# A two-layer graph network on one core: the walk over the edges in steps of one tile of 128 instead of two

## The chip, the core and the metric

The kernel runs on one core of a Trainium2 chip. The core has five engines that run side by side and meet through semaphores: TensorE (PE in the profile; PEld is its weight load), VectorE (DVE), ScalarE (ACT), GpSimd (POOL) and SyncE (SP), and 16 DMA engines. The metric is the device time of one execution, in microseconds (us), lower being better.

## The reference

`x` has 6250 rows (nodes) of 256 numbers. There are 200000 edges, sorted by their target node `dst`. Two graph attention layers run over them, and a linear attention ("mix") and a mixture of experts come with them:

```python
def gat_conv(x, W, a_src, a_dst, bias, src, dst, heads, out_ch, concat):
    h = (x @ W).reshape(n, heads, out_ch)
    al_s = jnp.einsum('nhc,hc->nh', h, a_src)
    al_d = jnp.einsum('nhc,hc->nh', h, a_dst)
    logits = jax.nn.leaky_relu(al_s[src] + al_d[dst], NEG_SLOPE)
    m = jax.ops.segment_max(logits, dst, num_segments=n)
    e = jnp.exp(logits - m[dst])
    denom = jax.ops.segment_sum(e, dst, num_segments=n)
    msg = h[src] * (e / denom[dst])[:, :, None]
    out = jax.ops.segment_sum(msg, dst, num_segments=n)
...
xn = _layernorm(x)
x = x + gnn(xn, edges) + mix(xn)          # gnn: gat_conv with 4 heads of 128, prelu, gat_conv with 1 head of 256
x = x + ffn(_layernorm(x))                # top 2 of 8 experts, hidden 1024
```

## The kernel before

The program has five passes, one after the other. `first_pass` normalises `x`, multiplies it by `W1`, and builds the tables of the edge walk. `walk_pass` runs for layer 1 (walk 1, 4 heads, rows of 528 numbers) and, after `finish_layer1`, for layer 2 (walk 2, 1 head, rows of 264 numbers). `finish_layer2` and `expert_pass` end the program.

**The walk's steps.** The nodes are cut into 49 windows of 128 (`NW`). The edge list is cut into blocks of `TPS * 128` edges, and one step of the walk is one block seen from one window: a block that spans the border of two windows is walked twice. So there are `STEPS = BLOCKS + NW - 1` steps. With `TPS = 2` these are 782 + 48 = 830 steps of two tiles of 128 edges. Ten steps (`CS`), that is 20 tiles (`CT`), make a chunk, and there are 83 chunks (`CHUNKS`), so 1660 tiles.

**What a chunk c goes through.** GpSimd gathers the source rows of its 20 tiles into a ring, one indirect DMA for each tile (line 871). The ring holds 2 chunks in walk 1 and 3 in walk 2 (`RS`); a gather waits until TensorE has multiplied the tile that stood in its place. ScalarE copies, for each step, the target window's terms into `goal` (`goals`, line 897); it first loads the ten window numbers of the chunk into registers (`windows_of`, line 714). TensorE spreads these to the edges (line 944). When all rows of chunk c+1 have landed, VectorE takes the maximum with them (`terms`, `walk_best`, line 1195), and a chain of small products and scans between TensorE and VectorE (lines 951 to 1239: `turn_best`, `scan_tiles`, `take_ends`, `scan_ends`, `bring_carry`, `scan_through`, `turn_peaks`, `gaps`) gives the softmax exponents `walk_gap` of chunk c+1. ScalarE turns them into weights and scales three of the four heads of each tile (walk 2: the one head), line 906; VectorE scales the fourth head in walk 1 (line 1260). VectorE also builds `walk_hit`, the 0/1 matrix that says which node of the window an edge belongs to (line 1244), and `walk_hitT` (line 1185).

**Multiply and add.** TensorE multiplies `hit` by the scaled rows of each step and sums both tiles of the step in one PSUM buffer (`multiply`, line 1047), 520 columns wide in walk 1 and 258 in walk 2; there are three such buffers (`PBUF`). VectorE adds each buffer into the accumulator `acc` of the step's window (`add`, line 1277; for the first step of a chunk, in parts with a rescale, lines 1268 to 1275). Each add waits for two semaphores: `multiplied`, for its own product, and `added`, which the add before it increments when it is complete:

```python
def add(c, i, r, s, w):
    b = (r * CS + s) % PBUF
    dve.wait_ge(multiplied, c * CS + s + 1 + AHEAD)
    dve.wait_ge(added, c * CS + s + PBUF)
```

The order of all this work on each engine is written out by hand in `chunk`. While VectorE adds chunk c, it works the chain of chunk c+1 in between. Before the first add of a chunk it loads that chunk's window numbers into registers. In walk 2 the mix (`mix_step`, `mix_products`, `roots`) is interleaved: through the first 50 chunks its keys, then its base rows.

Of the kernel before, what the change touches and what calls it, by code (L numbers as in the profile page):

```python
# [10 lines left out]
ALU = mybir.AluOpType  # L11
# [3 lines left out]
BF16 = mybir.dt.bfloat16  # L15
# [14 lines left out]
TPS = 2  # L30
# [17 lines left out]
CT = CS * TPS  # L48
CHUNKS = -(-STEPS // CS)
# [101 lines left out]
def first_pass(nc, k, d):  # L151


    with ExitStack() as ctx:
# [55 lines left out]
        tables = [a[:, 0:TPS * P] for a in (pF, pE)]  # L210
        XP = 10
        XPARTS = [(c, min(c + XP, NT)) for c in range(0, NT, XP)]
        TABLES = [(j, n) for j in range(SJ) for n in range(3)]
# [36 lines left out]
        with nc.Block() as block:  # L250

            @block.sync
            def _(sp):
# [35 lines left out]
                sp.wait_ge(tables_out, 16 * 10)  # L289
# [51 lines left out]
            def _(dve):  # L341
# [105 lines left out]
                def edge_step(n):  # L447
# [16 lines left out]
                    if n in (6, 7):  # L464
                        for way in range(2):
                            nc.vector.tensor_reduce(through[:, way, :, n - 6], reset[:, :, (n - 6) * P + way:(n - 5) * P + way], AX_X, ALU.min)
                        dve.drain()
                    if n == 7:
                        dve.sem_inc(resets_ready, 1)

                def copy_table(q):
                    j, n = TABLES[q]
                    dve.wait_ge(table_turned, q + 1)
                    steps = slice(j * P, (j + 1) * P)
                    to = (meta[:, 0, steps, :], meta[:, 1, steps, :], index[:, steps, :])[n]
                    nc.vector.tensor_copy(to.rearrange("p s u -> p u s"), tables[q % 2].rearrange("p (u s) -> p u s", u=TPS)
                                          ).then_inc(table_copied, 1)
# [32 lines left out]
            def _(pe):  # L510
# [8 lines left out]
                def edge_work(t):  # L519
# [6 lines left out]
                    if T_TURN <= t < T_TURN + len(TABLES):  # L526
                        q = t - T_TURN
                        j, n = TABLES[q]
# [5 lines left out]
                        for u in range(TPS):  # L534
                            last = nc.tensor.transpose(tables[q % 2][:, u * P:(u + 1) * P], (place, last_one, src)[n][:, j, u * P:(u + 1) * P],
                                                       k["ident"][:, :])
# [25 lines left out]
def walk_pass(nc, k, d, layer, H, A, F, attn, acc, table):  # L562
# [11 lines left out]
    WROW = CS  # L574
# [3 lines left out]
    AHEAD = RS * CS  # L578
    PBUF = 3
    HBUF = 3  # L580
    assert CHUNKS * CS >= STEPS and CHUNKS * CS <= SP
    assert TURN % RS == 0 and TURN % TS == 0 and TURN % IS == 0 and TURN * CS % PBUF == 0 and TURN * CGROUPS % HBUF == 0
    with ExitStack() as ctx:
# [7 lines left out]
        goal = m.sb("goal", [P, CS, 3, 2 * H], BF16)  # L591
# [8 lines left out]
        row_back = m.sb("row_back", [1, RK + 1])  # L600
        carry = m.sb("carry", [RK, 2])
        pair = m.sb("pair", [P, 2, H, CT + 1])
        gap = m.sb("gap", [P, H, CT + 1])
# [108 lines left out]
        def windows_of(engine, r):  # L712

            return nc.values_load_multi_w_load_instructions(win[0:1, r % IS, 0:CS], engines=[engine], min_val=0, max_val=NW - 1,
# [44 lines left out]
        with nc.Block() as block:  # L759

            @block.sync
            def _(sp):
# [5 lines left out]
                def load_tables(c, r):  # L768
# [3 lines left out]
                    sp.dma_start(win[:, r % IS:r % IS + both, 0:CS],  # L772
                                 d["windows"].unsqueeze(0)[:, bass.ds(c * CS, both * CS)].rearrange("o (c s) -> o c s", s=CS)
                                 ).then_inc(tables_ready(r), 16)

                def load_places(n):
                    sp.dma_start(hitT[:, :], d["places"][0:CHUNKS * CS, :].rearrange("(c s) e -> c (s e)", s=CS)[bass.ds(n, 1), :].to_broadcast([W, CT * P])
# [65 lines left out]
                def follow(c, i, r):  # L843
                    after(sp, gap_ready, c + 1)
                    load_resets(c + 2, r)
                    sp.wait_ge(added, c * CS + PBUF)
# [12 lines left out]
                if mixing:  # L859
                    for q in range(XB):  # L860
# [3 lines left out]
            def _(pool):  # L864
                def gather(c, i, r):
                    pool.wait_ge(index_ready(r), index_of(i, r))
                    for s in range(CS):
                        pool.wait_ge(multiplied, c * CS + s + 1)
                        pool.sem_inc(index_seen, 1)
                        for t in range(s * TPS, (s + 1) * TPS):  # L870
# [6 lines left out]
            def _(act):  # L877
# [12 lines left out]
                def goals(n, i, r):  # L890
# [5 lines left out]
                    for s in range(CS):  # L896
                        last = nc.scalar.copy(goal[:, s, :, :], target[:, at[s], :, :])  # L897
                    last.then_inc(goals_in, 1)

                def scale(c, i, r, s):  # L900
                    act.wait_ge(weights_ready, c + 1)
                    for t in range(s * TPS, (s + 1) * TPS):
# [32 lines left out]
            def _(pe):  # L935
                def spread_targets(n, i, r):
# [5 lines left out]
                    for s in range(CS):  # L942
                        for t in range(s * TPS, (s + 1) * TPS):
# [1291 lines left out]
```

## Time and profile before

| what | value |
|---|---|
| median of three runs | 5648.19 us (5645.58 to 5658.97) |
| the profiled execution | 5653.59 us, span 5651.8 us |
| walk 1, first chunk's first add to the last chunk's | 223.7 to 2329.4 us |
| walk 2, the same | 2565.1 to 4647.1 us |
| busy share of the span | PE 77%, PEld 59%, DVE 54%, ACT 53%, POOL 65% |
| gathers | 3320 instructions, 3200.0 us busy |

A row of the timeline gives start, duration, engine, line, operation, output and inputs, shape and count; the bracket is the idle time of the engine just before it and what ended it. "<-issue" is a wait that no event of the profile explains. A row of the waits gives total time, number and longest. "DVEq" is VectorE's own instruction queue, which handles register loads.

### The profile page before, as it was taken

The numbers are of one execution on the slowest core, as the hardware profiler recorded it, in microseconds if no ns is written. First come the engines' busy times: TensorE is split into PE (matmuls) and PEld (weight loads), VectorE is DVE, ScalarE is ACT, GpSimd is POOL, SyncE is SP. The second block draws the span as 40 slices with busy tenths as digits, with TensorE's granted clock in tenths as the row PEclk, the third lists the DMA queues.
The fourth block names the chain that finished last, engine by engine and source line by source line (L and its number), as shares of the span: only waits on it lengthen the run. The fifth ranks groups of instructions, "written<-read, shape, count | busy, mean of one in ns | idle before, by whom it ended". The sixth has DMA issues, their size and how long they took to land. (4 is left out here: it accounts for less than half of the span.)

```text
span 5651.8 us, 82730 instructions
## 1 busy us (share of the span) xinstructions
PE 4335.7 (77%) x21069; PEld 3336.5 (59%) x21069; DVE 3078.8 (54%) x8587; ACT 3010.0 (53%) x10079; POOL 3660.6 (65%) x3778
## 2 busy tenths in 40 slices
PE   7588888888888888775766667666565656899998
PEld 4466666666666666553444444444444435788887
DVE  5477777777777777654545545454454548211111
ACT  2677777777777777674545455453333334122221
POOL 0577777777777777457777777777777762344443
PEclk9789899999999998897778777787777775999999
DMA  5788878888888888435455444444556547443332
GB/s 188 236 242 242 243 234 244 241 243 241 243 243 244 240 243 238 144 119 145 138 143 143 138 144 138 143 140 140 170 159 171 159 119 238 143 129 129 127 127 74
DMA packets 427478, 1021.41 MB, mean 181 GB/s; under 512 B 115224, under 2 KB 207632, under 8 KB 426758
## 3 DMA queue, kind: packets, MB, share of 16 engines
q0 software_dynamic: 229312, 718.64, 44.4%
q1 hardware_dynamic: 197142, 296.44, 15.7%
q8 instruction: 181, 2.97, 0.2%
q14 instruction: 283, 2.32, 0.1%
q10 hardware_dynamic: 560, 1.05, 0.1%
HBM read 952.23 MB, written 65.48 MB: 180 GB/s over the span
## 5 line engine op out<-in xcount | busy, mean ns | idle before, releaser
L871 POOL DMA_INDIRECT walk_ring<-s_h,walk_index x3320 | 3200.0, 964 | 1169.5 <-issue 936.7
L1047 PE MATMUL walk_pM<-walk_ring,walk_hit 128*128 128x262 f32 (+1 forms) x9960 | 2776.8, 431 | 29.6 <-DVE acc L1275 18.0
L1047 PEld LDWEIGHTS walk_pM<-walk_ring,walk_hit 128*128 128x128 f32 x9960 | 2024.2, 211 | 449.9 <-issue 73.5
L906 ACT ACTIVATE walk_ring<-walk_ring 128x128 f32<-128x128 f32 (+1 forms) x6640 | 2134.3, 414 | 5.4
L1277 DVE TENSOR_TENSOR acc<-walk_pM,acc 128x520 f32 (+1 forms) x1494 | 834.3, 558 | 584.9 <-PE walk_pM L1047 564.4
L886 ACT ACTIVATE walk_ring<-walk_gap 128x40 f32<-128x40 f32 (+1 forms) x249 | 54.1, 259 | 1664.9 <-DVE walk_gap L1239 1664.9
L951 PE MATMUL walk_pC<-all_ident,walk_best 128*84 128x128 f32 (+1 forms) x166 | 61.7, 372 | 1032.2 <-DVE walk_best L1195 1032.2
L951 PEld LDWEIGHTS walk_pC<-all_ident,walk_best 128*84 128x84 f32 (+1 forms) x166 | 20.5, 124 | 1094.6 <-issue 1094.6
L1244 DVE TENSOR_TENSOR walk_hit<-walk_pK,walk_meta 128x512 f32<-128x512 f32 x830 | 561.1, 676 | 11.8
L2075 ACT ACTIVATE expert_hT<-expert_pH,expert_b 128x256 f32<-128x256 f32 x448 | 188.1, 471 | 594.7 <-PE expert_pH L2126 594.7
L1195 DVE TENSOR_TENSOR walk_best<-walk_ring,walk_dt 128x40 f32<-128x40 f32 (+1 forms) x249 | 47.1, 217 | 735.3 <-DMA walk_ring<-s_h,walk_index 735.2
L2126 PE MATMUL expert_pH<-expert_xT,expert_w 128*128 128x256 f32 x1792 | 397.5, 380 | 1.7 <-issue 1.7
L2138 PE MATMUL expert_pO<-down,expert_hT 128*128 x1792 | 395.9, 379 | 0.0
L2126 PEld LDWEIGHTS expert_pH<-expert_xT,expert_w 128*128 128x128 f32 x1792 | 341.4, 191 | 48.9 <-issue 2.3
L2138 PEld LDWEIGHTS expert_pO<-down,expert_hT 128*128 128x128 f32 x1792 | 336.3, 190 | 43.5
L2050 POOL DMA_INDIRECT out_dram<-expert_total,all_token_out x112 | 113.8, 1016 | 313.1 <-DVE expert_total L2092 306.8
L1260 DVE TENSOR_TENSOR walk_ring<-walk_ring,walk_pK 128x512 f32<-128x512 f32 x415 | 279.8, 674 | 0.1
L2083 DVE COPY expert_xT<-expert_pX 128x512 f32<-128x512 f32 x56 | 38.7, 692 | 361.9 <-PE expert_pX L2115 361.9
L897 ACT COPY walk_goal<-walk_target 128x24 bf16 (+1 forms) x1660 | 190.3, 199 | 39.3 <-issue 39.2
L2087 DVE TENSOR_TENSOR expert_out<-expert_pO,expert_b 128x256 f32<-128x256 f32 x112 | 47.6, 425 | 293.0 <-PE expert_pO L2138 293.0
L2045 POOL DMA_INDIRECT expert_total<-out_dram,all_token_in x112 | 107.6, 961 | 139.0 <-DMA out_dram<-expert_total,all_token_out 117.9
L2037 POOL DMA_INDIRECT expert_xin<-s_y,all_token_in x112 | 107.5, 959 | 126.4 <-POOLq L99 91.9
(320 smaller groups left out, 4030.1 us busy)
## 6 DMA issues: line engine op xcount, KB each, us to landing
walk_hitT<-s_places SPq DMA_DIRECT2D x166, 640.0 KB, 5.5
expert_w<-in_fw_dram SPq DMA_DIRECT2D x56, 1024.0 KB, 5.4
walk_ring<-s_h,walk_index POOLq DMA_INDIRECT x3320
walk_xk<-s_xT SPq DMA_DIRECT2D x98, 128.0 KB, 4.3
down<-in_fw_dram SPq DMA_DIRECT2D x8, 1024.0 KB, 11.8
s_h<-first_h_out SPq DMA_DIRECT2D x7, 1056.0 KB, 4.3
finish_rows<-s_h SPq DMA_DIRECT2D x7, 1056.0 KB, 6.2
walk_resets<-s_resets SPq DMA_DIRECT2D x82, 84.0 KB
```

What stands on the lines that cost most here:

```text
L871: pool.indirect_dma_start(ring[:, r % RS, t, :], None, table, bass.IndirectOffsetOnAxis(ap=index[:, r % TS, t:t + 1], axis=0)).then_inc(ro ...
L897: last = nc.scalar.copy(goal[:, s, :, :], target[:, at[s], :, :])
L906: last = nc.scalar.activation(row, row, ACT.Copy, scale=ring[:, r % RS, t, at + FH:at + FH + 1])
L1047: last = nc.tensor.matmul(pM[:, b, a, 0:WIDE], hit[:, (r * CGROUPS + g) % HBUF, t % GROUP, :], ring[:, r % RS, t, a * HALF_ROW:a * HALF_RO ...
L1244: nc.vector.tensor_tensor(hit[:, (r * CGROUPS + g) % HBUF, :, :], spread(count, 1, GROUP), spread(meta[:, 0, r % IS, g * GROUP:(g + 1) * G ...
L1260: nc.vector.tensor_tensor(rows, rows, spread(weight_k[:, g * GROUP:(g + 1) * GROUP], 2, FH), ALU.mult).then_inc(dve_scaled, 1)
L1277: nc.vector.tensor_tensor(to, pM[:, b, :, 0:OUT], to, ALU.add).then_inc(added, 1)
L2045: pool.indirect_dma_start(total[:, h % 4, :], None, d["out"], bass.IndirectOffsetOnAxis(ap=k["token_in"][:, h:h + 1], axis=0)).then_inc(to ...
L2050: pool.indirect_dma_start(d["out"], bass.IndirectOffsetOnAxis(ap=k["token_out"][:, h:h + 1], axis=0), total[:, h % 4, :], None, bounds_che ...
L2075: nc.scalar.activation(hT[:, t % 2, c, :], pH[:, j, c % HB, :], ACT.Gelu, bias=b1[:, e, c:c + 1]).then_inc(h_ready, 1)
L2126: last = nc.tensor.matmul(pH[:, j, c % HB, :], w1[:, t % WS, kk, c * P:(c + 1) * P], xT[:, t % 2, kk, :], start=(kk == 0), stop=(kk == DK ...
L2138: last = nc.tensor.matmul(pO[:, q, 0:D], hT[:, t % 2, c, q * P:(q + 1) * P], w2[:, e, c, :], start=(c == 0), stop=(c == HC - 1))
```

## The change

`TPS` goes from 2 to 1. A block is one tile of 128 edges, there are 1563 blocks and 1563 + 48 = 1611 steps, and a chunk still has 20 tiles; it now has 20 steps. `CHUNKS` is 81, so there are 1620 tiles in each walk. Each tile has a PSUM buffer and an add of its own, and `PBUF` stays 3. The old grouping in twos lives on as `PART = 2` in the order of the work: `add` now does the two adds of a part one behind the other. The first pass gathers 13 blocks of edges per partition instead of 7, and turns as many tables as before (two at a time). `gap` and `row_back` share memory with `pair`.

```diff
-TPS = 2
+TPS = 1
...
-CHUNKS = -(-STEPS // CS)
+PART = 2
+CT = CS * PART
+CHUNKS = -(-STEPS // CT)
...
-            return nc.values_load_multi_w_load_instructions(win[0:1, r % IS, 0:CS], ...)[1]
+            return nc.values_load_multi_w_load_instructions(win[0:1, r % IS, 0:CT], ...)[1]
...
-                    for s in range(CS):
-                        last = nc.scalar.copy(goal[:, s, :, :], target[:, at[s], :, :])
+                    for t in range(CT):
+                        last = nc.scalar.copy(goal[:, t, :, :], target[:, at[t], :, :])
...
-                    for u in range(TPS):
-                        t = s * TPS + u
+                    for t in range(s * PART, (s + 1) * PART):
+                        pe.wait_ge(added, c * CT + t + 1)
                         for a in range(A):
-                            last = nc.tensor.matmul(pM[:, b, a, 0:WIDE], hit[...], ring[...], start=(u == 0), stop=(u == TPS - 1))
-                    last.then_inc(multiplied, 1)
+                            last = nc.tensor.matmul(pM[:, (r * CT + t) % PBUF, a, 0:WIDE], hit[...], ring[...], start=True, stop=True)
+                        last.then_inc(multiplied, 1)
...
-                def add(c, i, r, s, w):
-                    b = (r * CS + s) % PBUF
-                    dve.wait_ge(multiplied, c * CS + s + 1 + AHEAD)
-                    dve.wait_ge(added, c * CS + s + PBUF)
+                def add(c, i, r, s, at):
+                    for t in range(s * PART, (s + 1) * PART):
+                        add_tile(c, i, r, t, at[t])
+
+                def add_tile(c, i, r, t, w):
+                    b = (r * CT + t) % PBUF
+                    dve.wait_ge(multiplied, c * CT + t + 1 + AHEAD)
+                    dve.wait_ge(added, c * CT + t + PBUF)
```

On VectorE, at the border of two chunks of walk 1, the program before has these rows (an ISA row sets the address registers of the add behind it, and its waits are the add's):

```order
L1244 TENSOR_TENSOR walk_hit<-walk_pK,walk_meta 128x512 [waits walk1_multiplied,walk1_tables_in1]
L1260 TENSOR_TENSOR walk_ring<-walk_ring,walk_pK 128x4x128
L1277 ISA [waits walk1_added,walk1_multiplied]
L1277 TENSOR_TENSOR acc<-walk_pM,acc 128x520
L1277 ISA [waits walk1_added,walk1_multiplied]
L1277 TENSOR_TENSOR acc<-walk_pM,acc 128x520
L1244 TENSOR_TENSOR walk_hit<-walk_pK,walk_meta 128x512 [waits walk1_multiplied,walk1_tables_in1]
L1260 TENSOR_TENSOR walk_ring<-walk_ring,walk_pK 128x4x128
L714 TENSOR_LOAD walk_win
```

The changed program has these in the same place, from behind the same `walk_ring` row on:

```order
L1281 ISA [waits walk1_added,walk1_multiplied]
L1281 TENSOR_TENSOR acc<-walk_pM,acc 128x520
L1281 ISA [waits walk1_added,walk1_multiplied]
L1281 TENSOR_TENSOR acc<-walk_pM,acc 128x520
L1281 ISA [waits walk1_added,walk1_multiplied]
L1281 TENSOR_TENSOR acc<-walk_pM,acc 128x520
L1281 ISA [waits walk1_added,walk1_multiplied]
L1281 TENSOR_TENSOR acc<-walk_pM,acc 128x520
L1244 TENSOR_TENSOR walk_hit<-walk_pK,walk_meta 128x512 [waits walk1_multiplied,walk1_tables_in1]
L1260 TENSOR_TENSOR walk_ring<-walk_ring,walk_pK 128x4x128
L714 TENSOR_LOAD walk_win
```

The two adds of steps 8 and 9 have become four in a row, each waiting for `added` from the one before it; the register load now takes 20 numbers. Everywhere else in the chunk one add has become two in a row.

On TensorE, around the wait for `walk_best` in the middle of a chunk of walk 1, before:

```order
L1047 MATMUL walk_pM<-walk_ring,walk_hit 128x262 [waits walk1_act_scaled,walk1_added]
L1047 MATMUL walk_pM<-walk_ring,walk_hit 128x262 x3
L951 MATMUL walk_pC<-all_ident,walk_best 84x128 [waits walk1_best_ready]
L1047 MATMUL walk_pM<-walk_ring,walk_hit 128x262 [waits walk1_hits_ready,walk1_dve_scaled,walk1_act_scaled,walk1_added]
L1047 MATMUL walk_pM<-walk_ring,walk_hit 128x262 x3
L956 MATMUL walk_pC<-all_ident,walk_ahead_max 1x84 [waits walk1_tiles_scanned]
```

And in the changed program:

```order
L1047 MATMUL walk_pM<-walk_ring,walk_hit 128x262 [waits walk1_added,walk1_act_scaled]
L1047 MATMUL walk_pM<-walk_ring,walk_hit 128x262
L1047 MATMUL walk_pM<-walk_ring,walk_hit 128x262 [waits walk1_added]
L1047 MATMUL walk_pM<-walk_ring,walk_hit 128x262
L952 MATMUL walk_pC<-all_ident,walk_best 84x128 [waits walk1_best_ready]
L1047 MATMUL walk_pM<-walk_ring,walk_hit 128x262 [waits walk1_dve_scaled,walk1_added,walk1_hits_ready,walk1_act_scaled]
L1047 MATMUL walk_pM<-walk_ring,walk_hit 128x262
L1047 MATMUL walk_pM<-walk_ring,walk_hit 128x262 [waits walk1_added]
L1047 MATMUL walk_pM<-walk_ring,walk_hit 128x262
```

The products are the same. A wait for `added` now stands before every tile instead of every second one, and with three buffers TensorE can be three tiles ahead of VectorE's adds instead of six.

## Rows read from the trace of the kernel before

**Rows 1.** The walks: length, busy PE, PEld, DVE, ACT, POOL; clock, DMA share, GB/s.

```profile
223.00:2329.00 2106.00, 1798.69 (x9022) 1415.14 (x9021) 1547.80 (x3935) 1574.04 (x5975) 1568.45 (x1627) 0.91 0.80 240
2565.00:4647.00 2082.00, 1334.78 (x6446) 932.02 (x6445) 1031.03 (x3224) 937.91 (x2811) 1571.22 (x1632) 0.77 0.52 147
```

**Rows 2.** GpSimd: one gather in the timeline, then its waits in walk 1.

```profile
1001.71 0.94 POOL L871 DMA_INDIRECT walk_ring<-s_h,walk_index  x1 [0.30 <-issue]
...
POOL walk_ring L871 <- PE walk_pM L1047: 76.8, 221, 2.0
```

**Rows 3.** VectorE's waits in walk 1: us, times, longest.

```profile
DVE acc L1277 <- PE walk_pM L1047: 235.9, 250, 2.6
DVE walk_best L1195 <- DMA walk_ring<-s_h,walk_index: 216.6, 81, 4.8
DVE walk_rescale L1268 <- issue: 28.6, 41, 1.0
DVE acc L1277 <- DVE acc L1277: 17.2, 78, 0.6
```

**Rows 4.** VectorE's waits in walk 2, the same columns.

```profile
DVE walk_best L1195 <- DMA walk_ring<-s_h,walk_index: 495.7, 82, 11.2
DVE acc L1277 <- PE walk_pM L1047: 322.2, 290, 2.5
DVE walk_ssum L1111 <- ACT walk_square L913: 94.5, 49, 3.0
```

**Rows 5.** VectorE's timeline between two chunks of walk 1, twice.

```profile
1022.05 0.69 DVE L1277 TENSOR_TENSOR acc<-walk_pM,acc 128x520 f32 x1
1022.96 0.70 DVE L1277 TENSOR_TENSOR acc<-walk_pM,acc 128x520 f32 x1 [0.21 <-DVE acc L1277]
1023.57 0.68 DVE L1244 TENSOR_TENSOR walk_hit<-walk_pK,walk_meta 128x512 f32<-128x512 f32 x1
1024.17 0.68 DVE L1260 TENSOR_TENSOR walk_ring<-walk_ring,walk_pK 128x512 f32<-128x512 f32 x1
1025.53 0.16 DVE L1268 TENSOR_SCALAR walk_rescale<-walk_pM 128x4 f32<-128x4 f32 x1 [0.68 <-issue]
...
1051.18 0.15 DVE L1268 TENSOR_SCALAR walk_rescale<-walk_pM 128x4 f32<-128x4 f32 x1
```

**Rows 6.** First and last chunk's first add, walks 1 and 2, timeline.

```profile
223.74 0.16 DVE L1268 TENSOR_SCALAR walk_rescale<-walk_pM 128x4 f32<-128x4 f32 x1 [3.59 <-PE walk_pM L1047]
...
2329.38 0.16 DVE L1268 TENSOR_SCALAR walk_rescale<-walk_pM 128x4 f32<-128x4 f32 x1
...
2565.13 0.16 DVE L1268 TENSOR_SCALAR walk_rescale<-walk_pM 128x1 f32<-128x1 f32 x1 [2.38 <-PE walk_pM L1047]
...
4647.11 0.16 DVE L1268 TENSOR_SCALAR walk_rescale<-walk_pM 128x1 f32<-128x1 f32 x1 [0.29 <-issue]
```

**Rows 7.** Register loads on VectorE's queue: L714 twice, then L2101 (one number).

```profile
L714 DVEq TENSOR_LOAD <-walk_win x1: 2290/2290/2290, 1023.1 to 1023.1; - x1
...
L714 DVEq TENSOR_LOAD <-walk_win x1: 1076/1076/1076, 1049.5 to 1049.5; - x1
...
L2101 DVEq TENSOR_LOAD <-all_expert x56: 298/304/321, 4853.4 to 5630.1; - x56
```

**Rows 8.** TensorE's timeline around its wait for best, two chunks.

```profile
1033.59 0.41 PE L951 MATMUL walk_pC<-all_ident,walk_best 128*84 128x128 f32 x1 [3.34 <-DVE walk_best L1195]
1033.84 3.83 PE L1047 MATMUL walk_pM<-walk_ring,walk_hit 128*128 128x262 f32 x8
...
2314.84 0.28 PE L951 MATMUL walk_pC<-all_ident,walk_best 128*84 128x128 f32 x1 [1.69 <-DVE walk_best L1195]
2315.10 2.01 PE L1047 MATMUL walk_pM<-walk_ring,walk_hit 128*128 128x262 f32 x8
```

**Rows 9.** Walk 2: the second of two adds in a row on VectorE, and ScalarE's scaling.

```profile
4619.50 0.43 DVE L1277 TENSOR_TENSOR acc<-walk_pM,acc 128x258 f32 x1 [0.21 <-DVE acc L1277]
...
3019.58 8.09 ACT L906 ACTIVATE walk_ring<-walk_ring 128x256 f32<-128x256 f32 x20
```

More of the change, by code:

```diff
@@ L533, in edge_work @@
                             pe.wait_ge(table_copied, q - 1)
-                        for u in range(TPS):
-                            last = nc.tensor.transpose(tables[q % 2][:, u * P:(u + 1) * P], (place, last_one, src)[n][:, j, u * P:(u + 1) * P],
+                        for u, j in enumerate(js):
+                            last = nc.tensor.transpose(tables[q % 2][:, u * P:(u + 1) * P], (place, last_one, src)[n][:, j, 0:P],
                                                        k["ident"][:, :])
@@ L941, in spread_targets @@
                     pe.sem_inc(part_seen, 1)
-                    for s in range(CS):
-                        for t in range(s * TPS, (s + 1) * TPS):
-                            last = nc.tensor.matmul(spread_t[:, t * SPREAD:(t + 1) * SPREAD], hitT[:, t * P:(t + 1) * P],
-                                                    goal[:, s, :, :].rearrange("p a q -> p (a q)"), start=True, stop=True)
+                    for t in range(CT):
+                        last = nc.tensor.matmul(spread_t[:, t * SPREAD:(t + 1) * SPREAD], hitT[:, t * P:(t + 1) * P],
+                                                goal[:, t, :, :].rearrange("p a q -> p (a q)"), start=True, stop=True)
                     last.then_inc(spread_out, 1)
@@ L1043, in multiply @@
                             pe.wait_ge(dve_scaled, c * CGROUPS + g + 1)
-                    for u in range(TPS):
-                        t = s * TPS + u
+                    for t in range(s * PART, (s + 1) * PART):
+                        pe.wait_ge(added, c * CT + t + 1)
                         for a in range(A):
-                            last = nc.tensor.matmul(pM[:, b, a, 0:WIDE], hit[:, (r * CGROUPS + g) % HBUF, t % GROUP, :],
-                                                    ring[:, r % RS, t, a * HALF_ROW:a * HALF_ROW + WIDE], start=(u == 0), stop=(u == TPS - 1))
-                    last.then_inc(multiplied, 1)
+                            last = nc.tensor.matmul(pM[:, (r * CT + t) % PBUF, a, 0:WIDE], hit[:, (r * CGROUPS + g) % HBUF, t % GROUP, :],
+                                                    ring[:, r % RS, t, a * HALF_ROW:a * HALF_ROW + WIDE], start=True, stop=True)
+                        last.then_inc(multiplied, 1)
                 def chunk(c, i, r):
```

88 lines of the change are left out of this document (43 added, 45 removed).

## The prediction

> **What bounds the kernel now.** I read the windows of the profile first, then each walk's waits engine by engine, then the timeline of single chunks. The two walks take 4.2 of the 5.65 ms, and in both GpSimd starts 1627 to 1632 gathers [rows 1]. A gather is busy for 0.94 us and 0.30 us of issue stands before each [rows 2]; over walk 1 the busy mean is 1568.45 / 1627 = 0.964 us, so 20 gathers take about 25.3 us. A chunk takes as long: from the first chunk's first add to the last one's there are 82 chunk periods, (2329.4 - 223.7) / 82 = 25.68 us in walk 1 and (4647.1 - 2565.1) / 82 = 25.39 us in walk 2 [rows 6]. So the queue of gathers sets the pace, and VectorE waits for rows to land: 216.6 us in walk 1 and 495.7 us in walk 2 [rows 3, 4]. The reader should also see how little stands behind that in walk 1. Of each 25.68 us VectorE waits 2.64 for rows and 235.9 / 82 = 2.88 for TensorE's products [rows 3]; the other 20.16 us it works or is held up by its own issue. TensorE is busy for 1799 of 2106 us there [rows 1]. Walk 2 has room: 6.05 us a chunk of waiting for rows and 3.93 for products [rows 4].
>
> **The gathers.** Each walk loses 2 of 83 chunks. Where gathers stay the pace, that is 2 x 25.68 = 51 us in walk 1 and 2 x 25.39 = 51 us in walk 2.
>
> **The adds.** Each chunk gets 10 more adds on VectorE, of unchanged width since the shape of an add does not depend on the number of tiles summed. The question is what one more costs. From the start of one 520-wide add to the next instruction it is 0.61 us (1022.96 to 1023.57), but between two adds in a row it is 0.91 us (1022.05 to 1022.96), with 0.21 us of idle time put down to the first add [rows 5]; this occurs 78 times, 17.2 us in all [rows 3]. The code explains it: the second add waits on `added`, which the first one increments at its end, so it can't overlap the first one's tail. All 10 new adds stand right behind another add, so I take 0.91 us each: 9.1 us a chunk. In walk 2 the second add of a pair is 0.43 us with 0.21 us before it [rows 9]: 0.64 us, 6.4 a chunk.
>
> On this point the trace and the Trainium skill differ. Its page "VectorE: DVE Perf Modes", section "The DRAIN you can't avoid", measures a chain of copies with and without a semaphore after each and finds that "the semaphore costs nothing extra here". By it the price of an added add would be the 0.61 us alone. The measured pair has a wait as well as an increment, and I go by the measured pair.
>
> **The register load.** Before the first add of a chunk VectorE loads the window numbers. With ten numbers this takes 2.29 us in one chunk and 1.08 in the next, and a load of one number 0.30 [rows 7]. The long one shows as 0.68 us of idle before line 1268, the short one as none [rows 5]; it starts just behind the last add's start, so about 2.29 - 0.68 = 1.6 us of it lies under the hit and the scaling in front. The load of 20 numbers isn't in this trace. From 0.30 for one and 1.08 for ten, a number costs 0.086 us: 20 are 1.9 us. What makes every second load 1.2 us longer I take for a border in memory that ten numbers (40 bytes) cross in every second chunk; 80 bytes would cross one always. That gives 3.1 us and 1.5 us of idle. The bounds are 2.29 us (as the long one now: 0.7 idle) and twice the long one, 4.6 us (3.0 idle). I take 1.5, against 28.6 / 82 = 0.35 now [rows 3].
>
> **VectorE's period in walk 1.** 20.16 - 0.35 + 9.1 + 1.5 = 30.4 us. That is above the 25.3 of the gathers, so the wait for landed rows goes and VectorE is the bound. Do its waits for TensorE stay? I followed one chunk with TensorE at 1.0 us a tile (2.01 us for 8 matmuls [rows 8]) and its limit of three tiles ahead. Each tile is ready before VectorE comes to it, since the pair of adds takes 1.5 us and something of 0.6 to 2 us always stands between pairs; TensorE needs some 22.5 us for a chunk, and waits for VectorE in pieces of 1 to 2 us. So most of these waits should vanish. They now come from TensorE's own stop: it waits 3.3 us for `walk_best` and then takes 3.83 us for 8 matmuls, as at 1.2 instead of 2.4 GHz; after a stop of 1.69 us it takes 2.01 and has lost nothing [rows 8]. The new stops are of the second kind. ScalarE waits for the exponents in walk 1, not the reverse; ten more goal copies there are hidden. Walk 1 then takes 80 x 30.4 = 2432 us from first add to last add, against 2105.7: **+326**. With 0.7 us for the load it is 29.6 a chunk (+262); with 3.0 it is 31.9 (+446).
>
> **Walk 2.** VectorE's time without these three waits is (2082.0 - 495.7 - 322.2 - 94.5) / 82 = 14.3 us, of it 0.8 more for products at the first add. With 6.4 for the adds and 1.0 for the load it is about 21, under the 25.3 of the gathers. In the 49 chunks with keys VectorE also waits at the sum of squares for ScalarE (94.5 us now [rows 4]), which from the exponents on has 8.09 us of scaling [rows 9], its own longer register load, 20 goal copies and the squares, some 13 us, while VectorE needs some 9 from there: up to 4 us. Those chunks come to 25 us, and with half of today's waits for products to 26.8. I take 25.7 for them and 25.4 for the rest: 80 x 25.4 + 49 x 0.3 = 2047, against 2082: **-35**. The bounds are -50 (gathers set the pace in all) and +40 (26.9 us in the 49).
>
> **First pass.** Six more gathers of edges at 1.25 us [rows 2] and six more small counting steps on VectorE, 2 us, come to 9 us, mostly beside other work: **+3**, bounds 0 and 9. Chunk heads, the tail behind each last chunk, and the other passes stay.
>
> **The sum.** 5653.6 (the profiled execution) + 326 - 35 + 3 = 5948. The median of the runs stands 5.4 us below that execution: 5942, so I say 5940 us, 5% slower.
>
> **Rivals.** (1) The waits for TensorE stay beside the new adds, because with three tiles of lead instead of six both engines now wait for each other: the period is 30.4 + 2.9 = 33.3 us, walk 1 +558, total 6175. For it speaks that TensorE has a stop before nearly every pair; against it that it is quick enough in my chunk. It would come in parts, and each 1 us of waiting left is 80 us. (2) The other side, faster: the wait on the own semaphore costs nothing in a long row of adds, and the load of 20 numbers stays under cover. Then the period is 20.16 + 6.1 = 26.3, walk 1 is 80 x 26.3 = 2104, -2, and the total 5653.6 - 2 - 50 - 5.4 = 5596. Every one of 78 pairs speaks against it. It decides from there: up to 26.3 us a chunk walk 1 costs nothing, and the total stays under 5648 up to a period of 26.9. The page named above gives this case if its sentence holds for a wait too. (3) The gathers keep the pace in both walks and all 102 us come back, 5546: this needs VectorE's 10 adds in the 5.5 us it now waits, at 0.61 us they are 6.1 already, so it is nearly excluded. (4) No change: only between (2) and the forecast.
>
> **How the numbers follow.** The forecast has 0.73; rival 1, wholly or by more than half, 0.18; rival 2 and 3 0.05; and the narrow place between, or a period about 27, 0.04. The bounds of the forecast: 29.6 a chunk and -50 give 5860; no idle for the load at all, 28.9 a chunk, gives 5800; 31.9 a chunk with +40 gives 6138. Half of rival 1 gives 6060 on top of the central sum. The range 5830 to 6110 leaves about 2 in 10 outside, most of it above. A measurement of this kernel tells 0.3% (17 us) from no change. Slower by more has 0.93, within 0.3% 0.02, faster 0.05.
>
> **What the profile will show.** Adds: line 1281, 18 a chunk of 0.69 us in walk 1, half of them or more with 0.2 us before them put down to the add before. The period of the first add (line 1272) near 30.4 us in walk 1 and 25.4 in walk 2. VectorE's wait for landed rows near nothing in walk 1, and GpSimd waiting for TensorE about 5 us a chunk there. Register loads on VectorE's queue of 3.1 us, with 1.5 us of idle before line 1272. TensorE's clock in walk 1 no lower than today's 0.91. I am wrong if VectorE still waits more than 1 us a chunk for products in walk 1 (rival 1), if pairs of adds follow at 0.61 us (rival 2), or if walk 2's period leaves 25.3 to 26 us.

## The result, and the profile after

The changed kernel takes 5817.98 us (median of 4 runs, 5814.16 to 5819.27), the kernel before on the same chip 5653.58: a ratio of 1.0285, 95% interval 1.0272 to 1.0298. It is slower, as forecast, but by 164 us and not by 292: the time lies 12 us under the range. Some of the experiments below ran on two other chips, where the kernel before itself takes 6482 and 6561 us; their times are read only against the kernel before in the same runs.

The first add of the first and last chunk, walk 1 and then walk 2, in VectorE's timeline of the changed kernel (line 1272, line 1268 before [rows 6]):

```profile
235.99 0.16 DVE L1272 TENSOR_SCALAR walk_rescale<-walk_pM 128x4 f32<-128x4 f32 x1 [1.74 <-PE walk_pM L1047]
...
2532.61 0.15 DVE L1272 TENSOR_SCALAR walk_rescale<-walk_pM 128x4 f32<-128x4 f32 x1
...
2772.12 0.16 DVE L1272 TENSOR_SCALAR walk_rescale<-walk_pM 128x1 f32<-128x1 f32 x1 [1.36 <-PE walk_pM L1047]
...
4800.94 0.16 DVE L1272 TENSOR_SCALAR walk_rescale<-walk_pM 128x1 f32<-128x1 f32 x1 [0.57 <-PE walk_pM L1047]
```

With the two spans (5651.8 and 5812.4 us) they cut the difference of 160.6 us into five:

| stretch | before | after | difference | forecast |
|---|---|---|---|---|
| start to walk 1's first add | 223.7 | 236.0 | +12.3 | +3 |
| walk 1, to the last chunk's first add | 2105.7 | 2296.6 | +190.9 | +326 |
| between the walks | 235.7 | 239.5 | +3.8 | 0 |
| walk 2 | 2082.0 | 2028.8 | -53.2 | -35 |
| the rest | 1004.7 | 1011.5 | +6.8 | 0 |

Walk 1 now has a period of 2296.6 / 80 = 28.71 us, walk 2 one of 25.36 us. The windows of both walks, columns as in [rows 1]:

```profile
236.00:2532.60 2296.60, 1773.61 (x8808) 1239.26 (x8807) 2038.44 (x4639) 1628.18 (x6633) 1530.16 (x1587) 1.00 0.75 215
2772.00:4801.00 2029.00, 1447.01 (x6307) 861.37 (x6305) 1330.16 (x3953) 999.32 (x3544) 1528.17 (x1593) 0.82 0.52 147
```

VectorE is busy for 2038 of 2297 us in walk 1, where it was 1548 of 2106. Its waits there, with one row each of GpSimd and ScalarE:

```profile
DVE acc L1281 <- DVE acc L1281: 170.4, 793, 0.6
DVE acc L1281 <- DVE acc L1279: 17.3, 80, 0.6
DVE acc L1276 <- issue: 13.9, 80, 0.6
DVE acc L1281 <- PE walk_pM L1047: 3.2, 7, 0.6
DVE walk_best L1195 <- DMA walk_ring<-s_h,walk_index: 3.0, 1, 3.0
...
POOL walk_ring L873 <- PE walk_pM L1047: 250.9, 311, 2.0
...
ACT walk_ring L888 <- DVE walk_pairs L1239: 665.8, 80, 10.9
```

Against [rows 3] two waits are gone (235.9 us for products is 3.2, 216.6 us for rows is 3.0), and so is the issue wait before the chunk's first add. One has come: 793 adds, 10 a chunk, wait 0.21 us each for the add before them. The others wait for what hangs on VectorE: TensorE for its adds, and behind TensorE the gathers; ScalarE for its exponents. The end of a chunk of walk 1 in the timeline, which answers to [rows 5]:

```profile
1038.01 0.70 DVE L1281 TENSOR_TENSOR acc<-walk_pM,acc 128x520 f32 x1 [0.21 <-DVE acc L1281]
1038.92 0.70 DVE L1281 TENSOR_TENSOR acc<-walk_pM,acc 128x520 f32 x1 [0.21 <-DVE acc L1281]
1039.83 0.70 DVE L1281 TENSOR_TENSOR acc<-walk_pM,acc 128x520 f32 x1 [0.21 <-DVE acc L1281]
1040.44 0.68 DVE L1244 TENSOR_TENSOR walk_hit<-walk_pK,walk_meta 128x512 f32<-128x512 f32 x1
1041.04 0.68 DVE L1260 TENSOR_TENSOR walk_ring<-walk_ring,walk_pK 128x512 f32<-128x512 f32 x1
1041.64 0.16 DVE L1272 TENSOR_SCALAR walk_rescale<-walk_pM 128x4 f32<-128x4 f32 x1
```

Adds in a row start 0.91 us apart, as they did before. But line 1272 starts 0.60 us behind line 1260 with no gap. The register load of 20 numbers (count, shortest, median and longest in ns) is not the 3.1 us that I forecast:

```profile
L714 DVEq TENSOR_LOAD <-walk_win x162: 1346/1351/1624, 232.6 to 4799.5; - x162
```

Walk 2 still waits for rows, so the gathers set its pace:

```profile
DVE walk_best L1195 <- DMA walk_ring<-s_h,walk_index: 261.3, 79, 11.0
DVE acc L1281 <- DVE acc L1281: 127.8, 592, 0.6
```

### The profile page after: what moved, and what is told of

The parts are those of the page before. It is cut to its first block and busy times, and to the rows that moved or that the text cites. A ratio compares the mean times of both kernels' runs of the same rounds, so it can differ in the third digit from the quotient of the medians.

```text
span 5812.4 us, 89329 instructions
## 1 busy us (share of the span) xinstructions
PE 4426.8 (76%) x20706; PEld 3085.7 (53%) x20706; DVE 3878.2 (67%) x10049; ACT 3122.5 (54%) x11489; POOL 3585.2 (62%) x3704
## 5 line engine op out<-in xcount | busy, mean ns | idle before, releaser
L873 POOL DMA_INDIRECT walk_ring<-s_h,walk_index x3240 | 3117.5, 962 | 1381.0 <-issue 920.1
L1047 PE MATMUL walk_pM<-walk_ring,walk_hit 128*128 128x262 f32 (+1 forms) x9720 | 2872.8, 430 | 608.6 <-DVE acc L1281 441.3
L1047 PEld LDWEIGHTS walk_pM<-walk_ring,walk_hit 128*128 128x128 f32 x9720 | 1786.6, 203 | 1377.1 <-DVE acc L1281 713.1
L908 ACT ACTIVATE walk_ring<-walk_ring 128x128 f32<-128x128 f32 (+1 forms) x6480 | 2083.0, 414 | 5.3
L1281 DVE TENSOR_TENSOR acc<-walk_pM,acc 128x520 f32 (+1 forms) x3078 | 1717.3, 558 | 454.4 <-DVE acc L1281 301.6
L888 ACT ACTIVATE walk_ring<-walk_pairs 128x40 f32<-128x40 f32 (+1 forms) x243 | 52.7, 258 | 1672.3 <-DVE walk_pairs L1239 1672.3
L1244 DVE TENSOR_TENSOR walk_hit<-walk_pK,walk_meta 128x512 f32<-128x512 f32 x810 | 547.5, 676 | 11.5
L899 ACT COPY walk_goal<-walk_target 128x24 bf16 (+1 forms) x3240 | 356.3, 200 | 50.0 <-issue 49.8
```

Of the source, the lines that this page charges most:

```text
L873: pool.indirect_dma_start(ring[:, r % RS, t, :], None, table, bass.IndirectOffsetOnAxis(ap=index[:, r % TS, t:t + 1], axis=0)).then_inc(ro ...
L899: last = nc.scalar.copy(goal[:, t, :, :], target[:, at[t], :, :])
L908: last = nc.scalar.activation(row, row, ACT.Copy, scale=ring[:, r % RS, t, at + FH:at + FH + 1])
L1047: last = nc.tensor.matmul(pM[:, (r * CT + t) % PBUF, a, 0:WIDE], hit[:, (r * CGROUPS + g) % HBUF, t % GROUP, :], ring[:, r % RS, t, a * HA ...
L1244: nc.vector.tensor_tensor(hit[:, (r * CGROUPS + g) % HBUF, :, :], spread(count, 1, GROUP), spread(meta[:, 0, r % IS, g * GROUP:(g + 1) * G ...
L1281: nc.vector.tensor_tensor(to, pM[:, b, :, 0:OUT], to, ALU.add).then_inc(added, 1)
```

## The experiments

### Is it VectorE's adds in a row? (e1_spread)

The work and every wait are those of the changed kernel; only VectorE's order differs.

```diff
-                    add(c, i, r, 0, at)
...
+                    tile(0)
                     hits(c, i, r, 2)
+                    tile(1)
                     scale(c, i, r, 2)
-                    add(c, i, r, 1, at)
+                    tile(2)
+                    scale(c, i, r, 3)
+                    tile(3)
...
```

> The changed kernel with the same work and the same waits, but the two adds of a part no longer stand in a row: a hit, a scaling or a link of the chain stands between them wherever there is one. Of about 11 adds a chunk that stand right behind another, 3 are left. If the wait on the own increment is a latency that other work covers (theory: each add in a row costs 0.91 instead of 0.61 us, and VectorE sets the period in walk 1), 8 x 0.30 = 2.4 us a chunk go: period of the first add in walk 1 from 28.7 to 26.3 us, 80 x 2.4 = 192 us in all, total near 5626 us. If the 0.3 us are a fixed price of the wait wherever it stands, or if TensorE or ScalarE set the period: 28.7 us and 5818 us. If the new order makes TensorE's products late (they come in other gaps): between, with VectorE waiting for TensorE. In walk 2 nothing, gathers set the pace there.

Measured: 5642.17 us, ratio 0.9971 (0.9959 to 0.9982); run again (e1_third, below), 5641.80, 0.9975 (0.9965 to 0.9985). Its timeline, first and last chunk of walk 1, and three rows inside a chunk, then what is left of the self-waits in walk 1:

```profile
238.75 0.16 DVE L1279 TENSOR_SCALAR walk_rescale<-walk_pM 128x4 f32<-128x4 f32 x1 [1.74 <-PE walk_pM L1047]
...
1011.49 0.69 DVE L1288 TENSOR_TENSOR acc<-walk_pM,acc 128x520 f32 x1
1012.10 0.68 DVE L1267 TENSOR_TENSOR walk_ring<-walk_ring,walk_pK 128x512 f32<-128x512 f32 x1
1012.69 0.69 DVE L1288 TENSOR_TENSOR acc<-walk_pM,acc 128x520 f32 x1
...
2357.48 0.16 DVE L1279 TENSOR_SCALAR walk_rescale<-walk_pM 128x4 f32<-128x4 f32 x1
```

```profile
DVE acc L1288 <- DVE acc L1288: 35.4, 161, 0.6
```

The period is (2357.5 - 238.7) / 80 = 26.48 us: 2.2 us under 28.71, where 2.4 were expected. With a scaling between them the second add starts 1.20 us behind the first, 0.60 us for the add and 0.60 for the scaling: the wait costs nothing there. So the 0.30 us are a latency that 0.6 us of other work covers, and VectorE's time was the period. The profile still names 161 self-waits, where it had 793. This settles the main term, and in this order steps of one tile are no longer a loss.

### Does the shorter lead of TensorE matter? (e5_pbuf2)

```diff
-    PBUF = 3
+    PBUF = 2
```

> The changed kernel with 2 product buffers instead of 3. Rival 1 of the prediction was that a lead of three tiles is too short, so that VectorE waits for TensorE. If VectorE alone sets the period with room to spare, two tiles of lead still do in most places: VectorE's waits for products at the adds rise from 3 us to some 80 us in walk 1 (1 us a chunk), total 5818 to 5900. If three was already near the edge, each pair of adds waits for its second product, about 0.5 us x 10 a chunk: 80 x 5 = 400 us, total near 6200 us. No change at all: the lead has no part in the time.

Measured: 5848.90 us, ratio 1.0335 (1.0318 to 1.0353), 31 us over the changed kernel; period 29.05 us. VectorE's waits in its walk 1:

```profile
DVE acc L1281 <- DVE acc L1281: 138.2, 638, 0.6
DVE acc L1281 <- PE walk_pM L1047: 59.9, 164, 1.0
```

A lead of two tiles brings back 0.75 us a chunk of waits for products, part of which falls into the self-waits. At three tiles it is 0.04 us. Rival 1 had the right mechanism and began one buffer lower.

### What makes a register load long? (e3_win22, e4_before_win12)

```diff
-    WROW = CT
+    WROW = CT + 2
```

> The changed kernel with the rows of the window-number tile 22 numbers (88 bytes) apart instead of 20 (80 bytes); 20 are loaded as before. Theory: a register load is slow when its row does not start on a multiple of 16 bytes; rows 1 and 3 of four then start at 88 and 264 bytes, every second load on VectorE takes 2.5 us or more instead of 1.35 us, and since 1.6 us of it is covered, 0.9 us or more of idle time stands before line 1272 in every second chunk: walk 1 gets 40 x 0.9 = 36 us longer, total near 5855. Rival (what I took in the prediction, a border that the row crosses): 80 bytes always cross one and cost nothing for it, so there is no such thing, all loads stay at 1.35 us and the time at 5818.

Measured: 5941.45 us, ratio 1.0499 (1.0481 to 1.0516). Two loads in a row on VectorE's queue, and its wait before the first add in walk 1:

```profile
L714 DVEq TENSOR_LOAD <-walk_win x1: 1362/1362/1362, 1026.8 to 1026.8; - x1
...
L714 DVEq TENSOR_LOAD <-walk_win x1: 4501/4501/4501, 1055.3 to 1055.3; - x1
```

```profile
DVE walk_rescale L1272 <- issue: 116.5, 40, 3.3
```

The direction is the theory's; the size was too small. Every second load, the one whose row starts 8 bytes past a multiple of 16 (counted from the start of the tile), takes 4.5 us instead of 1.36 here, and 116.5 / 40 = 2.9 us of it are bare. Walk 1 becomes 2417.0 us long, 30.2 a chunk, 120 more than the changed kernel's, and that is nearly the whole loss of 123 us. Walk 2 stays at 2030.2 us though its loads are as long, since it waits for rows anyway. The counterpart, in the kernel before:

```diff
-    WROW = CS
+    WROW = CS + 2
```

> The kernel before (two tiles a step), with the rows of its window-number tile 12 numbers (48 bytes) apart instead of 10 (40 bytes); ten are loaded as before (the small tiles reset0 and ratio share one allocation to make room). Theory: what makes every second load on VectorE 2.29 instead of 1.08 us is a row that starts off a multiple of 16 bytes, so all loads take about 1.08 us now. Rival (the border I assumed): rows at 48 and 96 bytes still cross a multiple of 64 bytes, so two of four stay long. For the time both say the same: the idle time before line 1268 in walk 1 falls from 28.6 us to about 5 under the theory, but gathers set the pace there, so it turns into waiting for rows and the total stays at the 5656 us of before, within 5 us.

Measured on a chip where the kernel before takes 6481.81 us: 6495.72, ratio 1.0019 (1.0007 to 1.0030), 14 us more where no difference beyond 5 us was expected. All loads on VectorE's queue, in the kernel before on the first chip and then in this one:

```profile
L714 DVEq TENSOR_LOAD <-walk_win x166: 1060/1213/2320, 218.5 to 4645.9; - x166
...
L714 DVEq TENSOR_LOAD <-walk_win x166: 1060/1066/1323, 245.3 to 5503.3; - x166
```

Rows of 48 bytes have only short loads, though two of four cross a multiple of 64 bytes; rows of 40 bytes had 2.29 us in every second chunk [rows 7]. The chip is not the reason: the loads of the kernel e7_again below have a median of 1351 ns on such a chip too, as in the changed kernel on the first. The changed kernel itself speaks against the border: each of its rows of 80 bytes crosses a multiple of 64, and all its loads are short. The border that I assumed is refuted, the alignment stands. All slow rows start 8 bytes past a multiple of 16; other offsets were not tried.

### Where did 12 us in the first pass go? (e2_through_pool, e8_third)

SyncE's queue in the changed kernel, then DMA and engines over 14 us behind it (window columns as in [rows 1]):

```profile
120.52 5.99 SPq L273 DMA_DIRECT2D s_through<-first_through  x2
126.55 1.67 SPq L285 DMA_DIRECT2D s_h<-first_h_out  x1
128.27 2.69 SPq L286 DMA_DIRECT2D s_xT<-first_xT  x1
```

```profile
126.00:140.00 14.00, 4.97 (x24) 2.92 (x22) 2.80 (x13) 1.05 (x4) 0.00 (x0) 0.82 1.01 27
```

The 16 DMA engines are full and move only 27 GB/s, all stores together. What stands in front on the queue is `through`, the table of resets over a whole tile, whose store goes element by element: 2 x 1664 pieces of 4 bytes now, where two tiles a step made 2 x 896 pieces of 8 bytes. The store of `xT` behind it lands 19.4 us after its issue, the next one after 4.2 us, and everything stops for it: ScalarE needs the buffer, then TensorE, then VectorE. ScalarE's wait in the first pass (sum, times, longest), and VectorE's timeline at the stall, in the changed kernel and then in the kernel before:

```profile
ACT first_xT L323 <- DMA s_xT<-first_xT: 22.7, 4, 19.1
```

```profile
152.49 0.17 DVE L502 COPY all_attn<-first_pA 128x8 f32<-128x8 f32 x1 [21.15 <-PE first_pA L556]
...
137.25 0.17 DVE L503 COPY all_attn<-first_pA 128x8 f32<-128x8 f32 x1 [10.31 <-PE first_pA L557]
```

So the kernel before has this stall too, half as long: 10.8 us more are the change's. All such waits of the first pass together are 65.9 us before and 77.1 after, 11.2 of the 12.3 us.

First I gave the two stores to GpSimd's queue:

```diff
+                pool.wait_ge(resets_ready, 1)
+                for way in range(2):
+                    pool.dma_start(d["through"][way, :].rearrange("(j p u) -> p j u", p=P, u=TPS), through[:, way, :, :], ...
...
```

> The changed kernel, but the two stores of the table through (elements of 4 bytes, 1664 of them each) are issued by GpSimd on its own queue instead of by SyncE, in the same part of the first pass. Theory: of the 12.3 us that walk 1 starts later, nearly all is SyncE's queue standing behind these stores, so that the store of xT lands late and ScalarE and TensorE wait for the buffer (one wait of 21.2 us where before had one of 10.3): the first add of walk 1 comes at 224 to 228 us instead of 236, total 8 to 12 us lower, near 5807. Rival: the time is that of the 16 DMA engines working through small elements, whoever issues them: the same stall, 236 us and 5818. Rival: it comes from the six more gathers of edge blocks (7.5 us later tables): 236 us too, without the long wait.

Measured: 5809.63 us, ratio 1.0267 (1.0249 to 1.0284); first add at 231.6 us, neither the 224 to 228 of the theory nor the 236 of the rivals. A stall of 12.99 us stays in place of 21.15, and the waits together are 70.7 us, so 6.4 of the 11.2 us are gone. But the stall now ends at 119.5 us instead of 152.5: the stores moved in time as well as to another queue, and this run doesn't part the two. Then the same table in rows of 52 bytes, which leaves out the right order of its values and shows only the time:

```diff
-                            sp.dma_start(d["through"][way, :].rearrange("(j p u) -> p j u", p=P, u=TPS), ...
+                            sp.dma_start(d["through"][way, :].rearrange("(p j u) -> p j u", p=P, u=TPS), ...
```

> The kernel e8_through_rows once more (through in rows of 52 bytes, in another order than the walk expects). On a usual chip: first gather of walk 1 near 183 us instead of 194.5, first add 224 to 228 us instead of 236, total 8 to 12 us under after_third, if small elements make the stall; no difference otherwise.

Measured beside the changed kernel on one chip: 5800.07 us, ratio 1.0253 (1.0235 to 1.0270), and 5820.98 for the changed one, 1.0291 (1.0274 to 1.0308): 21 us less. The same window, ScalarE's wait, and walk 1's first add in the timeline:

```profile
126.00:140.00 14.00, 13.06 (x62) 8.05 (x61) 5.07 (x23) 4.80 (x16) 0.00 (x0) 1.00 0.75 251
```

```profile
ACT first_xT L322 <- DMA s_xT<-first_xT: 7.3, 4, 2.8
```

```profile
222.38 0.16 DVE L1271 TENSOR_SCALAR walk_rescale<-walk_pM 128x4 f32<-128x4 f32 x1 [1.73 <-PE walk_pM L1046]
```

251 GB/s instead of 27 in the same 14 us, and the walk starts 13.6 us earlier than in the result's profile (17.2 before that of the second one), earlier even than before the change. So the small pieces make the stall. The start is 1.3 us earlier than before, but the waits for these products are 61.3 us against 65.9, so about 3 us of something else came in, which may be the six gathers more of edge blocks. The start itself varies: seven traces with the changed kernel's first pass have it at 236.0 to 241.1 us.

### Is VectorE alone above the gathers' pace? (e7_third, e9_best, e10_share3)

e7_third is the kernel e7_share (its first runs come below). It starts from e1_spread, and `GA = 3` says that ScalarE scales the fourth head of the last two groups of tiles, and the chain is cut finer between adds. Against e1_spread:

```diff
+    GA = 3
...
-                        for h in range(HA):
+                        for h in range(HA if t // GROUP < GA else H):
...
                     tile(2)
-                    scale(c, i, r, 3)
+                    if n:
+                        goal_terms(*n)
...
```

> The kernel e7_share once more. On a usual chip: VectorE sets the period: 25.3 us a chunk in walk 1, total near 5548 us, VectorE waiting for rows in walk 1 again; or ScalarE is the next bound, 26 us or more, total 5600 or more. On a slow chip: 1.009 to 1.012 of the kernel before, as there.

Measured: 5585.31 us, ratio 0.9875 (0.9858 to 0.9891). Walk 1's first and last first add, and VectorE's waits in it:

```profile
237.13 0.16 DVE L1285 TENSOR_SCALAR walk_rescale<-walk_pM 128x4 f32<-128x4 f32 x1 [1.87 <-PE walk_pM L1048]
...
2283.11 0.16 DVE L1285 TENSOR_SCALAR walk_rescale<-walk_pM 128x4 f32<-128x4 f32 x1
```

```profile
DVE acc L1294 <- DVE acc L1294: 35.2, 162, 0.6
DVE walk_best L1203 <- DMA walk_ring<-s_h,walk_index: 24.0, 33, 3.1
```

The period is 25.57 us, and VectorE waits for rows again in 33 of 80 chunks: the bound has gone back to the gathers or close to them, 0.3 us a chunk above their 25.3. The total is 37 us above the 5548 expected. Walk 1 gained 0.9 and not 1.2 us a chunk, which is 22 us; and walk 2, which was to stay, became 15 us longer, 2048.9 us where e1_third has 2034.2. What in the new order costs that in walk 2 was not tried. A correct store of `through` (turned by one transpose on TensorE, 26 rows of 512 bytes) was added to it:

```diff
-                            sp.dma_start(d["through"][way, :].rearrange("(j p u) -> p j u", p=P, u=TPS), through[:, way, :, :], ...
...
+                            sp.dma_start(d["through"][way, :].rearrange("(j p) -> j p", p=P), through_t[way * SJ:(way + 1) * SJ, :]).then_inc(tables_out, 16)
```

> The kernel e7_share, with the table through turned on TensorE (one transpose of 128 x 26 and one copy more) and stored in rows of 512 bytes, 26 pieces, in its right order, behind the other tables. If the small elements were the whole stall, the first add of walk 1 moves from 237 to 221 to 226 us, and the total is 11 to 17 us under e7_third: near 5572 us. If the turned table comes too late (it is the last that the first pass stores), the walk's first loads wait for it and the gain is gone: 5585.

Measured: 5574.88 us, ratio 0.9854 (0.9839 to 0.9869), the first add at 219.4 us instead of 237.1. The 18 us of the first pass are plain in the traces, but the total gained less: walk 2 took 2053.9 us, 5 more, and the two ratios, from two chips, have intervals that overlap. A third group of tiles on ScalarE on top of that:

```diff
-    GA = 3
+    GA = 2
...
-                    scale(c, i, r, 2)
```

> The kernel e9_best, with the fourth head of three of the five groups of tiles on ScalarE instead of two: VectorE 0.60 us less a chunk and 0.30 more for one more add right behind another, ScalarE 4 x 0.29 = 1.2 us more, of the 2.8 us that it waits in a chunk of walk 1. If VectorE still sets the period (25.58 us), it is 25.3 us now and the total 20 us under e9_best. If the gathers' pace is reached or ScalarE takes over, no change or slower by up to 40 us, with TensorE waiting for ScalarE's scaling.

Measured: 5570.45 us, 0.9845 (0.9831 to 0.9858), with a period of (2268.2 - 220.9) / 80 = 25.59 us, where e9_best has 25.53; the 20 us expected did not come. VectorE waits for rows in 63 chunks, 46.7 us, where it was 30 and 19.7 in e9_best. Less work on VectorE brings nothing now. So with the new order, the share of ScalarE and the other store, steps of one tile are 1.5% faster than the kernel before. The kernel before was not given the same three, so how much of the 1.5% the step of one tile itself brings is not shown.

### The same on other chips, and what was repeated

> The spread order of the first experiment, and the fourth head of the last two of a chunk's five groups of tiles is scaled by ScalarE (8 more of its scalings of 0.29 us, 2.3 us) instead of VectorE (2 x 0.60 us); the chain's links are cut in smaller pieces that stand between adds, three adds a chunk still stand right behind another. If VectorE sets the period of walk 1 (26.5 us in the first experiment), it falls by 1.2 us to about 25.3 us, where the gathers (25.3 us) take over: 80 x 1.2 = 94 us less, total near 5548 us, and VectorE waits for rows again in walk 1. Rival: ScalarE, which waits 8.3 us a chunk for the exponents now, gets them 2.4 us sooner by the shorter period and works 2.3 us more; if its chain is the next bound the period stays at 26 us or more and the total at 5600 or above, with TensorE waiting for ScalarE's scaling.

Where the kernel before takes 6482 us it took 6566.62, ratio 1.0120 (1.0102 to 1.0138).

> The kernel e7_share, with the two stores of through issued by GpSimd as in e2_through_pool. If that brings the 4 to 8 us here too that it brought there: e7_share minus 4 to 8 us. If its gain was chance of that program's first pass: the same as e7_share.

6555.58 us, ratio 1.0106 (1.0089 to 1.0124).

> The changed kernel with the table through stored in rows of 52 bytes (its 13 numbers of a partition in one piece) instead of single elements of 4 bytes, so 128 pieces a store instead of 1664. The table's values then stand in other places than the walk expects: this leaves out the right order of through and shows only the time. Theory A (small elements keep the DMA engines busy, whoever issues them): the stall in the first pass (a wait of 21.2 us for a product on VectorE) goes, walk 1's first add comes at 222 to 226 us instead of 236, total about 12 us lower, near 5806. Theory B (the six more gathers of edge blocks and what they delay): the first add stays at 232 us or later.

6517.31 us, ratio 1.0050 (1.0033 to 1.0068). Three of these kernels ran again on a third chip, where the kernel before takes 6561 us:

> The kernel e7_share once more, on a chip where the kernel before takes its usual 5650 us. VectorE sets the period: 25.3 us a chunk in walk 1 and a total near 5548 us, with VectorE waiting for rows in walk 1 again. ScalarE is the next bound: 26 us or more a chunk, total 5600 or more, TensorE waiting for ScalarE's scaling.

6619.21 us, ratio 1.0088 (1.0072 to 1.0104).

> The kernel e7b_share_pool once more, on the same chip as e7_again: 4 to 8 us below it if GpSimd's issue of the stores of through helps here as it did in e2_through_pool, the same as it otherwise.

6608.81 us, ratio 1.0068 (1.0053 to 1.0084): 11 and 10 us under e7_share on the two chips, in line with e2_through_pool, but with intervals that overlap.

> The kernel e8_through_rows once more (through stored in rows of 52 bytes, in another order than the walk expects). Where small elements make the stall: no wait of over 4 us for a product on VectorE in the first pass, the first gather of walk 1 near 183 us instead of 194.5, its first add 224 to 228 us instead of 236, total 8 to 12 us under the changed kernel. Otherwise the first gather stays at 190 us or later.

6567.86 us, ratio 1.0005 (0.9992 to 1.0018). Three rows of e7_again's timeline of VectorE, within 30 us:

```profile
1045.39 0.70 DVE L1294 TENSOR_TENSOR acc<-walk_pM,acc 128x520 f32 x1 [3.35 <-remote]
...
1057.70 0.15 DVE L1221 COPY walk_pC<-walk_row_ahead 1x4 f32<-1x4 f32 x1 [3.53 <-remote]
...
1075.14 0.16 DVE L1285 TENSOR_SCALAR walk_rescale<-walk_pM 128x4 f32<-128x4 f32 x1 [3.40 <-remote]
```

These waits, which the profile puts down to nothing of this core, and waits of 2.4 us for products stand there at places where none are on the first chip. The gathers' own time is not longer (955 ns on average from 1000 to 2000 us, 966 in e7_third), but the period of walk 1 is 31.9 us instead of 25.57. So these runs don't answer the questions. All four kernels then ran on one chip where the kernel before takes 5654.17 us; e7_third and e8_third stand above, the other two were:

> The changed kernel itself. On a chip where the kernel before takes 5650 us: 1.028 of it, 5818 us, period 28.7 us in walk 1. On a chip where the kernel before takes 6480 to 6560 us: e8_through_rows, the same but for one table, was 1.0005 and 1.005 of it there, so 1.002 to 1.007. That would say that what slows the kernel before there (waits of about 2.4 us that products of TensorE come late by) has taken the pace from the gathers and from VectorE.

5820.98 us, ratio 1.0291 (1.0274 to 1.0308).

> The spread order once more. On a usual chip 0.997 of the kernel before, as measured. On a slow chip: if the self-wait still counts there, below after_third; if late products of TensorE set the pace, the same as after_third or above it, since less VectorE work in a row is nothing then.

5641.80 us, ratio 0.9975 (0.9965 to 0.9985). Both repeat what they gave at first.

## Why the prediction was right in direction and wrong in size

**The gathers.** Right. Two chunks fewer bring 53 us in walk 2, where gathers are the pace (51 forecast).

**The adds.** Right, and the term that decides. (Line 1281 runs 19 times a chunk, not 18.) Each new add costs 0.91 us in walk 1; 10 a chunk stand right behind another. Rival 2 is refuted by 793 self-waits in the trace and by e1_spread, which takes most of them away and gets 2.2 us a chunk back. The sentence of the Trainium skill, page "VectorE: DVE Perf Modes", section "The DRAIN you can't avoid", that the semaphore "costs nothing extra here", holds in e1_spread, where other work stands between increment and wait (0.60 us an instruction); it doesn't for an instruction that waits for the increment of the one right before it (0.91 us). By it alone the period would have been 26.3 us, near the 26.48 of e1_spread.

**The register load.** This step failed: "That gives 3.1 us and 1.5 us of idle." The load takes 1.35 us and leaves no idle time, and the 0.35 us a chunk that were there have gone too. Both parts of the 3.1 us were too large: ten more numbers on an aligned row add 0.28 us (1.07 to 1.35) and not 0.86, and the 1.2 us for a border don't come. Without the term the sum gives 20.16 - 0.35 + 9.1 = 28.9 us a chunk where 28.71 were measured. It was 1.5 x 80 = 120 us of the 133 us by which span and forecast differ (5946 and 5812 us); the rest is 15 us in walk 1 and 18 in walk 2 that I had too much, and 20 too little in the other stretches. The data of before fitted two rules, a border crossed and an alignment missed, and I took the one by which the change makes things worse. The other bound (none idle, 5800 in all) stood in the text, and the range left it out. e3_win22 comes out at the numbers that I had forecast, with 30.2 us a chunk and 5941 us, but by 2.9 us of idle time in every second chunk and not by 1.5 in each; that the means agree is chance.

**The waits for TensorE.** Right: 3 us left in walk 1, and its granted clock there is 1.00 where it was 0.91, so at the higher level throughout. Rival 1 doesn't occur at three buffers and begins at two.

**Walk 2.** -53 against -35. The 49 chunks with keys don't fall behind the gathers; ScalarE holds VectorE up for 88.9 us at the sum of squares, 94.5 before [rows 4], and that stays under cover. The upper bound was added up wrong: 31 x 25.4 + 49 x 26.9 = 2105 us is +24, not +40, and 6138 would be 6122; the stated range doesn't hang on it.

**The first pass.** A term mis-sized, +3 for +12.3. I counted gathers and small VectorE steps and overlooked a store by single elements whose pieces had become twice as many and half as large; its stall, 10.3 us before, grew to 21.2. Between the walks and behind them 3.8 and 6.8 us came that the sum had at 0; the ten more adds of each last chunk (9.1 and 6.4 us by the prices above) would be more than that in walk 1 and nearly all of it in walk 2; this was not followed further.

## What to carry to other kernels

Count a wait on the instruction just before as its own latency (0.3 us here), and put other work between (0.6 us was enough) before giving up a finer step: that order alone was worth 3%. Where one engine is to become the bound, find every fixed cost in front of its instructions and test the two or three rules that would fit it against the new sizes; a row moved off its alignment cost 2%. And look through the stores of a changed layout for the size of their pieces.

## What was unexpected of the hardware

- A register load of 20 numbers takes 1.35 us when its row starts at a multiple of 16 bytes and 4.5 us at 88 bytes; of ten numbers 1.07 us, and 2.29 us at 40 bytes. So twice the numbers on aligned rows cost a quarter more.
- With some 3300 pieces of 4 bytes in front, all 16 DMA engines were full for 14 us while 27 GB/s moved, and a store issued behind them took 19.4 us to land, where the next one took 4.2.
- The same kernel before takes 5654, 6482 and 6561 us on three chips, and the order of the kernels is not the same on them: e7_share is 1.2% faster than before on the first, 1.2% and 0.9% slower on the others. What the waits put down to "remote" are stays open.
